# A transformer block with its normalised rows turned in 32x32 blocks on VectorE and carried through HBM, in a new order of work

## What is computed

```python
nx = _ln(x, ln1_g, ln1_b)
q = (nx @ wq + bq).reshape(b, s, H, HD).transpose(0, 2, 1, 3)      # k, v alike
bias = jnp.where(adj_matrix > 0, 0.1 * edge_attr_matrix * adjf, -jnp.inf)[:, None]
scores = jnp.einsum('bhqd,bhkd->bhqk', q, k) / np.sqrt(HD) + bias
attn = jax.nn.softmax(scores, axis=-1)
out = jnp.einsum('bhqk,bhkd->bhqd', attn, v)
x1 = residual + (out @ wo + bo)
n2 = _ln(x1, ln2_g, ln2_b)
mlp = jax.nn.gelu(n2 @ w1 + b1, approximate=False) @ w2 + b2
return x1 + mlp
```

## Time and profile before

| | us |
|---|---|
| median of 3 runs | 1409.81 |
| lowest and highest | 1408.53, 1409.89 |
| the profiled execution, its time | 1407.88 |
| the same, span from first to last instruction | 1406.1 |
| TensorE, VectorE busy | 1354.4, 1190.3 |
| ScalarE, GpSimd busy | 1135.5, 559.5 |

### The profile page before, as it was taken

The page is one execution under the profiler, slowest core; times in us unless marked ns, Lnnn a source line. Parts: engine busy times, 40 slices in busy tenths (PEclk is TensorE's granted clock), DMA queues, the critical chain, the costliest instruction groups (busy, mean ns, idle before and its releaser), DMA issues.

```text
span 1406.1 us, 34020 instructions
## 1 busy us (share of the span) xinstructions
PE 1354.4 (96%) x11580; PEld 1165.4 (83%) x11580; DVE 1190.3 (85%) x2002; ACT 1135.5 (81%) x3336; POOL 559.5 (40%) x553
## 2 busy tenths in 40 slices
PE   7579999999999999999999999999999999999998
PEld 6468888888888888888888888888888888888876
DVE  3888988888898888898888899888889888889862
ACT  3678888888889888888888888988888988888753
POOL 3343334443334443333444333444333444433321
PEclk9889999999999999999999999999999999999999
DMA  4343334443333434333444333443433344433330
GB/s 150 113 142 122 126 123 138 145 137 131 126 121 125 153 127 146 130 112 126 143 142 142 119 128 123 134 152 127 140 130 115 119 153 141 142 120 121 101 118 23
DMA packets 147256, 180.15 MB, mean 128 GB/s; under 512 B 13584, under 2 KB 130576, under 8 KB 147216
## 3 DMA queue, kind: packets, MB, share of 16 engines
q1 hardware_dynamic: 147216, 179.63, 39.3%
HBM read 95.69 MB, written 83.89 MB: 128 GB/s over the span
## 4 chain that ended last, share of the span: by engine, by line
PE 91%; ACT 5%; DVE 2%; DMA 1%; issue 1%; POOL 0%; SPq 0%; ACTq 0%; DVEq 0%; POOLq 0%
PE work L376 27%; PE work L378 25%; PE work L377 25%; PE area L432 6%; PE work L478 4%; PE work L452 4%; ACT qk_all L653 2%; ACT soft L610 1%; PE work L383 1%; ACT late_memory L677 0%; DVE soft L839 0%; DVE wa_raw L851 0%; ACT late_memory L688 0%; DMA wa_raw<-in_L_gnn_wq 0%; DVE soft L815 0%
## 5 line engine op out<-in xcount | busy, mean ns | idle before, releaser
L610 ACT ACTIVATE soft<-soft,nmax 128x128 f32<-128x128 f32 x1024 | 396.8, 394 | 5.1 <-DVE nmax L823 4.7
L1015 POOL TENSOR_TENSOR ve<-mv,eps 128x4 f32<-128x4 f32 x64 | 13.0, 203 | 771.0 <-DVE mv L888 664.7
L376 PE MATMUL work<-w_hi,hid_parts 128*128 128x256 f32 x1024 | 295.4, 288 | 1.4 <-ACT late_memory L688 1.1
L378 PE MATMUL work<-w_hi,hid_parts 128*128 128x256 f32 x1024 | 286.1, 279 | 0.0
L377 PE MATMUL work<-w_lo,hid_parts 128*128 128x256 f32 x1024 | 285.9, 279 | 0.0
L924 DVE TENSOR_TENSOR hid_parts<-late_memory,hid_parts 128x512 fp32r<-128x512 f32 x256 | 224.9, 880 | 21.8 <-ACT hid_parts L698 21.6
L688 ACT ACTIVATE late_memory<-work,b_col 128x512 f32<-128x512 f32 x256 | 171.9, 684 | 69.9 <-PE work L378 53.8
L376 PE MATMUL work<-nt_hi,w_hi 128*128 128x512 f32 x512 | 211.7, 414 | 3.9 <-DVE nt_lo L914 3.8
L376 PEld LDWEIGHTS work<-w_hi,hid_parts 128*128 128x128 f32 x1024 | 191.9, 187 | 12.0 <-DVE xt_lo L914 5.8
L377 PE MATMUL work<-nt_lo,w_hi 128*128 128x512 f32 x512 | 201.3, 393 | 0.0
L378 PE MATMUL work<-nt_hi,w_lo 128*128 128x512 f32 x512 | 200.5, 392 | 0.0
(11 more groups left out here) (93 smaller groups left out, 3074.2 us busy)
## 6 DMA issues: line engine op xcount, KB each, us to landing
moved_blocks<-wa_raw SPq DMA_DIRECT2D x128, 512.0 KB, 2.7
probt<-moved_blocks SPq DMA_DIRECT2D x512, 128.0 KB, 2.9
xin<-in_x SPq DMA_DIRECT2D x32, 512.0 KB, 3.9
out<-res SPq DMA_DIRECT2D x128, 128.0 KB, 2.1
adj_in<-in_adj SPq DMA_DIRECT2D x32, 256.0 KB, 2.9
res<-in_L_gnn_w SPq DMA_DIRECT2D x1, 1024.0 KB, 9.6
late_memory<-in_L_gnn_w SPq DMA_DIRECT2D x1, 1024.0 KB, 12.1
wa_raw<-in_L_gnn_wq SPq DMA_DIRECT2D x1, 256.0 KB, 3.9
```

What stands on the lines that cost most here:

```text
L376: pe.matmul(o, lhs_hi, rhs_hi, start=first, stop=False)
L378: return pe.matmul(o, lhs_lo, rhs_hi, start=False, stop=last)
L610: a = act.activation(soft[:, b % 2, h, :], soft[:, b % 2, h, :], ACT.Exp, bias=nmax[:, b % 2, h:h + 1], accum_out=rsum[:, b % 2, h:h + 1])
```

## The change

`flip` and the identity are gone. The normalised rows of a group, 128 partitions by 1024 numbers, are turned in 32x32 blocks by one instruction on VectorE (`flat_blocks`) into a buffer `flat`, sent to HBM (`send_flat`) and fetched from there by four DMAs into their new place (`fetch_flat`), for "xt" over `xhat` itself, for "nt" into `nraw`. Both kinds use the one `flat`. `flip_hi` now reads SBUF, and `flip_lo` is a product of two SBUF operands on GpSimd. The columns of the early biases are made before the first step. x is normalised one step earlier and up and down come one step later, so that the steps run from -3, and every engine has a new order.

```diff
-UNITS = [("mix", 0, -1, 3), ("nt", 0, -2, 0), ("nt", 1, -2, 1), ("qk", 2, 0, 2), ("qk", 3, 0, 0),
...
+UNITS = [("up", 1, -3, 0), ("proj", 0, -1, 3), ("up", 2, -3, 1), ("up", 3, -3, 2), ("mix", 1, -1, 3),
...
-PER_GROUP = {"down": GB, "v": 2, "qk": 4, "up": FC, "xt": DC, "nt": DC, "mix": GB, "proj": GB}
-FIRST, EARLY, LATE = -2, 4, 2
+PER_GROUP = {"down": GB, "v": 2, "qk": 4, "up": FC, "mix": GB, "proj": GB}
+FIRST, EARLY, LATE = -3, 6, 3
...
+        nraw = sb("nraw", [P, GB * D])
+        flat = sb("flat", [P, RPB, GB * DC, HD])
...
+        xraw = xhat[:, :, :].rearrange("p b d -> p (b d)")
+        bv_wide = nraw[:, 0:DC * P].rearrange("p (c a) -> p c a", c=DC)
...
+        moved_flat = {k: nc.dram_tensor(f"moved_{k}", (RPB, HD, RPB, BLK), F32, kind="Internal").ap() for k in ("xt", "nt")}
...
+            def send_flat(step, off, kind):
+                if not step.has(off):
+                    return
+
+                sp.wait_ge(flat_ready[kind], step.through(off, 1, 0))
+                sp.dma_start(moved_flat[kind].rearrange("i k j n -> (i k) (j n)"),
+                             flat[:, :, :, :].rearrange("p j m t -> p (j m t)")).then_inc(flat_sent[kind], 16)
+
+            def fetch_flat(step, off, kind):
+                if not step.has(off):
+                    return
+                raw = xraw if kind == "xt" else nraw[:, :]
+
+                sp.wait_ge(flat_sent[kind], step.through(off, 1, 0, 16))
+                for j in range(RPB):
+                    sp.dma_start(raw[j * HD:(j + 1) * HD, :].rearrange("p (i n) -> p i n", i=RPB),
+                                 moved_flat[kind][:, :, j, :].rearrange("i k n -> k i n")).then_inc(flat_landed[kind], 16)
...
-                fetch_blocks(step, -1, 1)
                 send_blocks(step, -1, 2)
-                load_adj(step, 2)
                 fetch_blocks(step, -1, 2)
                 send_blocks(step, -1, 3)
+                load_x(step, 2)
                 fetch_blocks(step, -1, 3)
-                store(step, -2, 0)
+                send_flat(step, -2, "nt")
+                send_flat(step, 2, "xt")
+                store(step, -3, 0)
+                fetch_flat(step, -2, "nt")
+                load_adj(step, 3)
+                fetch_flat(step, 2, "xt")
                 send_blocks(step, 0, 0)
-                store(step, -2, 1)
+                store(step, -3, 1)
                 fetch_blocks(step, 0, 0)
-                store(step, -2, 2)
                 send_blocks(step, 0, 1)
-                store(step, -2, 3)
-                load_x(step, 2)
+                fetch_blocks(step, 0, 1)
+                store(step, -3, 2)
+                store(step, -3, 3)
...
-            pe.wait_ge(ident_ready, 1)
+            early_columns()
...
-            def flip(step, off, kind, c):
-                if not step.has(off):
-                    return
-                src, ready = (xhat, xhat_ready) if kind == "xt" else (nhat, nhat_ready)
-                free(step, kind, c)
-                for b in range(GB):
-
-                    if c == 0:
-                        pe.wait_ge(ready, step.through(off, GB, b))
-                    mm = pe.transpose(work[:, bank_of(kind, c), b * P:(b + 1) * P],
-                                      src[:, b, c * P:(c + 1) * P], ident[:, :])
-                mm.then_inc(full[kind], 1)
...
+                score(step, 0, 0)
+                up(step, -3, 1)
+                project_out(step, -1, 0)
+                up(step, -3, 2)
...
+                score(step, 0, 2)
+                query_key(step, 1, 0)
+                down(step, -3, 0)
+                query_key(step, 1, 1)
+                project_out(step, -1, 2)
+                down(step, -3, 1)
+                query_key(step, 1, 2)
...
+                down(step, -3, 2)
+                down(step, -3, 3)
+                mix(step, 0, 0)
                 up(step, -2, 0)
...
-                dst = xt_hi if kind == "xt" else nt_hi
+                dst, raw = (xt_hi, xraw) if kind == "xt" else (nt_hi, nraw[:, :])
...
-                act.wait_ge(full[kind], step.through(off, DC, c))
-                act.activation(dst[:, c, :], work[:, bank_of(kind, c), :], ACT.Copy)\
-                   .then_inc(hi_taken[kind], 1)
+                act.wait_ge(flat_landed[kind], step.through(off, 1, 0, LAND))
+                act.activation(dst[:, c, :].rearrange("p (b i t) -> p b i t", b=GB, i=RPB),
+                               raw.rearrange("p (i b c t) -> p b i c t", i=RPB, b=GB, c=DC)[:, :, :, c, :],
+                               ACT.Copy).then_inc(hi_taken[kind], 1)
...
-                    need(act, full["xt"], step.through(off - 1, DC, DC - 1))
+                    need(act, taken["xt"], step.through(off - 1, DC, DC - 1))
...
-                    need(act, full["nt"], step.through(off - 1, DC, DC - 1))
+                    need(act, flat_ready["nt"], step.through(off - 1, 1, 0))
...
+                norm2(step, -2, 1)
+                norm2(step, -2, 2)
+                gelu(step, -3, 0)
+                norm2(step, -2, 3)
+                hidden_hi(step, -3, 0)
+                gelu(step, -3, 1)
...
+                gelu(step, -3, 4)
+                exponential(step, 0, 0, 1)
+                gelu(step, -3, 5)
...
-            def flip_lo(step, off, kind, c):
-                if not step.has(off):
-                    return
-                hi, lo = (xt_hi, xt_lo) if kind == "xt" else (nt_hi, nt_lo)
-
-                dve.wait_ge(hi_taken[kind], step.through(off, DC, c))
-                dve.tensor_tensor(lo[:, c, :], work[:, bank_of(kind, c), :], hi[:, c, :].bitcast(F32),
-                                  ALU.subtract).then_inc(taken[kind], 1)
-                if kind == "xt" and c == DC - 1 and step.at_first(off):
                     early_biases()
+
+            def flat_blocks(step, off, kind, other, other_off):
+
+                if not step.has(off):
+                    return
+                src, ready = (xhat, xhat_ready) if kind == "xt" else (nhat, nhat_ready)
+                need(dve, flat_sent[kind], step.through(off - 1, 1, 0, 16))
+                need(dve, flat_sent[other], step.through(other_off, 1, 0, 16))
+                if kind == "nt":
+                    need(dve, taken["nt"], step.through(off - 1, DC, DC - 1))
+                dve.wait_ge(ready, step.through(off, GB, GB - 1))
+                dve.transpose(flat[:, :, :, :], src.rearrange("p b d -> p (b d)")
+                              .rearrange("p (m j k) -> p j m k", j=RPB, k=HD)).then_inc(flat_ready[kind], 1)
...
+                stats1(step, 2)
...
+                hidden_lo(step, -3, 5)
+                flat_blocks(step, -2, "nt", "xt", 1)
                 attn_lo(step, -1, 2)
-                hidden_lo(step, -2, 5)
-                stats2_of(step, -1, 0)
-                hidden_lo(step, -2, 6)
-                add_edges(step, 0, 1)
-                hidden_lo(step, -2, 7)
+                flat_blocks(step, 2, "xt", "nt", -2)
+                hidden_lo(step, -3, 6)
+                hidden_lo(step, -3, 7)
...
+            def flip_lo(step, off, kind, c):
+                if not step.has(off):
+                    return
+                hi, lo, raw = (xt_hi, xt_lo, xraw) if kind == "xt" else (nt_hi, nt_lo, nraw[:, :])
+
+                pool.wait_ge(hi_taken[kind], step.through(off, DC, c))
+                pool.tensor_tensor(lo[:, c, :].rearrange("p (b i t) -> p b i t", b=GB, i=RPB),
+                                   raw.rearrange("p (i b c t) -> p b i c t", i=RPB, b=GB, c=DC)[:, :, :, c, :],
+                                   hi[:, c, :].bitcast(F32).rearrange("p (b i t) -> p b i t", b=GB, i=RPB),
+                                   ALU.subtract).then_inc(taken[kind], 1)
...
-                rstd_of_x(step, 1)
                 result_start(step, -2)
+                residual_start(step, 0)
+                flip_lo(step, 1, "xt", 1)
+                rstd_of_x(step, 2)
+                edges(step, 1)
+                flip_lo(step, -2, "nt", 0)
+                flip_lo(step, -2, "nt", 1)
+                flip_lo(step, 2, "xt", 0)
                 rstd_of_n(step, -1)
-                residual_start(step, 0)
-                edges(step, 1)
```

208 lines of the change are left out of this document (87 added, 121 removed), and 3 rows, old and new, of the table UNITS.

## The result

The changed kernel takes 1712.78 us (median of 4 runs, 1711.14 to 1719.86) against 1409.83 for the one before on the same chip: 1.2161 times as long, with a 95% interval of 1.2137 to 1.2184. The forecast was 1566, in a range of 1450 to 1630: the sign was right, the loop in part, the size was not. The profiled execution has a span of 1711.2 us.

What follows compares the result with a forecast made beforehand. The prediction took a loop over all engines through the x load as the bound, 45.1 us plus collisions, taken as 47: 138 + 27 x 47 + 77 + 80 = 1564 us of span, 1566 us forecast, range 1450 to 1630.

Steps and rivals of the forecast that it cites:

- the loop: Waits round all engines from hidden_lo 7 to the next step's, through the x load: 47 us a step; chance 0.70.
- the removed work: Sixteen transposes a step leave TensorE, 1.76 us; with nothing in their way steps would be 39.7 us instead of 41.5.
- the collisions: Two-input instructions of VectorE and GpSimd exclude each other for the whole instruction; put at 2.2 us in the loop.
- wait for the send: VectorE's flat_blocks "xt" waits until the one buffer flat has been sent: 2.7 us.
- the two starts: GpSimd's result_start and residual_start, back to back after norm2 3, 2.42 us each; only then may x be loaded.
- the x load is not late: Rival: GpSimd starts earlier, so a shorter loop without the x load decides, 43 to 44 us a step, 1466 us; chance 0.10.
- TensorE stays the bound: Rival: steps of 39.7 us, 1369 us in all, faster than before; chance 0.07.
- if the two engines alternate: Worst case of VectorE and GpSimd: block 3's turn and send, ahead of the x load, come 1.5 later; loop 48.8 us.
- worse than my bounds: Rival: collisions in more places, or TensorE's granted clock falling in its holes, over 1630 us; chance 0.11.
- steps without up and down last 30.1: At the start, three such steps instead of two, the third with the wait for flat; first full step near 138 us.
- The signs in the profile: Steps of 45 to 49 us, TensorE 81 to 88% busy, idle before bn_stats and xhat's transpose, hidden_lo means above 0.88 us.

Runs made afterwards that it cites:

- 20 and 6 idle products: Changed kernel with 20 idle 256-column TensorE products before the wait for hidden tile 6 and 6 before that for tile 7 in down 0: 1716.13 us.
- 10 and 2: Changed kernel with 10 and 2 idle 256-column TensorE products ahead of the waits for hidden tiles 6 and 7 in down 0: 1717.54 us.
- one-input starts: Changed kernel with GpSimd's result_start and residual_start as one-input multiplications by 1.0, biases bo and b2 left out of the output: 1641.14 us.

## Why the prediction was right and where it was wrong

**What bounds the kernel, and the removed work.** Right. Where little hinders it TensorE's step is near the 39.7 that the prediction gave it: 40.3, of which it is busy 98.8%, with the waits gone and the collisions shortened.

**The loop and its order.** Right from the load of x on: stats1, flat_blocks "nt", wait for the send, flat_blocks "xt", hidden_lo 6 and 7. Undoing its x part alone gave 7.2 of 9.5 us back. Ahead of the load it was wrong: the prediction lets the load follow norm2 3 and the two starts, and in the kernel after it follows hidden_lo 0 and 1, the turn of block 3 and its send, and goes out 2.35 us after the starts have ended. Only with the load ahead of that send (20 of 25 turns) or with one-input starts (25 of 25) does the last chain reach the load over the starts. The rivals "the x load is not late" and "TensorE stays the bound" are out: stats1 waits 128 us for its load, and TensorE is busy 43.3 of 51.1 us.

**The loop's terms.** This is the step that failed first: the wait of the load behind the turn of block 3, which the sum puts at nothing, and the collisions, which it puts at 2.2 us. The turn at 708.85 took 51.5 us, against 47 predicted and 45.1 without collisions. Its terms by the timeline, beside those of the 45.1:

| stretch | predicted | measured |
|---|---|---|
| hidden_lo 7 to result_start (708.85 to 735.27) | 24.8 | 26.4 |
| the two starts (to 741.24) | 4.8 | 6.0 |
| from there to the load of x (743.59) | 0 | 2.35 |
| landing (747.87) | 3.9 | 4.3 |
| stats1 to the end of flat_blocks "nt" (754.09) | 6.3 | 6.2 |
| wait for the send (756.84) | 2.7 | 2.75 |
| flat_blocks "xt", hidden_lo 6 and 7 (760.34) | 2.5 | 3.5 |

Against those 6.4 us I had set 2.2 for collisions. The largest difference is the third row. The prediction has it as "if the two engines alternate, the turn of block 3 and its send ... come 1.5 later", as the worst case and not as the value taken, and it was 2.35 (2.15 by the run that moves the load). The alternation itself was not in the starts' 4.8. One row of before, a hidden_lo delayed once by a product that ran already, was taken as the rule, but with two products queued on each side each waits for the other. The one-input run, in which a tile is still slowed to 1.43 us, prices what it takes away at 2.5 us a step. In the first row 1.6 us are TensorE at its 1.2 GHz level behind the hole. That the clock could fall in holes stood in the text as a rival, "worse than my bounds", with 0.11, and not as a term; it was worth up to 1.5 us in a turn. Whether that is a gain to be had stays open: with 20 and 6 idle products a step was some 0.6 us shorter in the profiled execution and the end took most of it back, and with 10 and 2 the low clock stood elsewhere.

**Start.** The second step that failed: "steps without up and down last 30.1; there are three now". From the load of x at 52.81 to that at 182.53 they took 129.7 us, where three of 30.1 and one wait of 2.7 make 93. The 30.1 came from steps of before in which the load of x was not in a loop; after, each of the three has the load, the rstd, and in their chain edges, on which the queue stood for the adjacency. The run with the adjacency loaded later takes 6 to 7 us of that away. The rest is not shown by a run, only argued: loads and sends in the chain, at a granted clock of 0.61, 0.67 and 0.75 in the windows 45.9:92, 92:133 and 133:179, where the two such steps of before had 0.90 (34:64) and 0.75 (64:94).

**The sum.** Of the 147 us between 1564 and 1711, 36.7 are in the first steps, 107 in the 26 steps from 182.53 to 1511.58 (1329 for 26 x 47 = 1222), and 3 in what is left, the time before 52.81 and the end, which came out near.

**The signs in the profile.** TensorE 85% busy (81 to 88 predicted), bn_stats idle 4.1 us (1 to 4, just over), the transposition of xhat 2.4 idle (2 to 2.5), hidden_lo 1.27 us (above 0.88): right, or nearly. Steps of 45 to 49: wrong, 51.1.

## What to carry to other kernels

Before a transfer is put between two stages of the same step, walk the loop once round with every wait in it, and give each its full price: what stands ahead on the queue, the buffer it shares, and the engines that take turns. The bounds of such a sum belong to all terms together, since a late instruction meets collisions that it used to miss, and a wait taken away can give more than its own length. When two paths meet at one instruction, price both: here the load waited for the longer one, and shortening the other gave little. And a gain on the bounding engine is worth something only where what it used to cover, here a hidden tile of 2.4 us, is gone as well; a deeper pipeline must earn back its ends.
